# The order of the sync engine's work in a softmax attention: load, maxima, stores

## The reference

```
xn  = layernorm(x)                                   # 8 x 512 x 128
q, k, v = split(xn @ w_qkv + b_qkv)                   # per sequence 16 heads of 8
p   = softmax(q @ k.T * 8 ** -0.5)                    # 512 x 512 for each of 128 heads
s   = concat_heads(p @ v) @ w_proj + b_proj
g   = silu(top-2-of-8 experts(xn))
x   = x + s * g
```

## Time and profile before

| | us |
|---|---|
| median of 3 runs | 1123.48 (1121.21 to 1131.17) |
| profiled execution, own time | 1125.44 |
| profiled execution, span of the core | 1123.7 |
| PE busy | 986.1 (88%) |
| VectorE busy | 843.9 (75%) |
| ScalarE busy | 625.0 (56%) |
| GpSimd busy | 583.7 (52%) |
| mean granted clock of PE | 0.918 |
| attention (first plain scores to last transposed ones) | about 36 to 465 |

### The profile page before, as it was taken

How to read it: one execution, slowest core, us unless ns; L and a number is a source line. 1 busy time by engine, 2 the same in 40 slices (tenths; PEclk the granted TensorE clock), 3 DMA queues, 4 the chain that set the end, 5 groups by cost and what they waited for, 6 DMA issues and landing times. The chain is left out here.

```text
span 1123.7 us, 21302 instructions
## 1 busy us (share of the span) xinstructions
PE 986.1 (88%) x5638; PEld 640.7 (57%) x5638; DVE 843.9 (75%) x1901; ACT 625.0 (56%) x1247; POOL 583.7 (52%) x645
## 2 busy tenths in 40 slices
PE   5789999999999999999999945989987999999960
PEld 4443343443434444387888835656555888888850
DVE  7757798999999998045445538597883999998975
ACT  6126688788888877633323316223333677767752
POOL 7221786334435440025555546288882577667770
PEclk9558799999999999999999975699998999999985
DMA  6736656435344531245665643022242676677728
GB/s 210 287 115 197 192 149 201 124 124 179 123 159 140 160 114 41 85 136 172 193 187 178 190 114 88 20 67 69 66 154 76 178 217 204 202 213 199 216 72 231
DMA packets 121472, 169.76 MB, mean 151 GB/s; under 512 B 18801, under 2 KB 80594, under 8 KB 118354
## 3 DMA queue, kind: packets, MB, share of 16 engines
q1 hardware_dynamic: 94290, 110.94, 33.9%
q0 software_dynamic: 18688, 54.08, 14.1%
q10 hardware_dynamic: 8448, 4.20, 1.5%
HBM read 106.71 MB, written 63.76 MB: 152 GB/s over the span
## 5 line engine op out<-in xcount | busy, mean ns | idle before, releaser
L1660 DVE TENSOR_REDUCE nmax<-ps 128x1 f32<-128x512 f32 x512 | 324.2, 682 | 48.6 <-PE ps L1028 43.9
L1297 ACT ACTIVATE stage<-ps 128x512 f32<-128x512 f32 x512 | 274.6, 594 | 74.1 <-PE ps L1022 65.8
L846 POOL DMA_INDIRECT token_y<-stage,ids_now x184 | 184.9, 1005 | 141.4 <-DVE stage L1716 62.3
L1028 PE MATMUL ps<-stage,stage 32*128 32x512 f32 x512 | 190.0, 512 | 12.2 <-DVE nmax L1660 10.7
L1168 PE MATMUL ps<-stage,stage 128*128 128x128 f32 (+1 forms) x1288 | 172.5, 277 | 7.3 <-DVE stage L1780 3.9
L1022 PE MATMUL ps<-stage,stage 32*128 32x512 f32 x512 | 170.8, 487 | 8.9 <-DMA stage<-q_halves 3.9
L1168 PEld LDWEIGHTS ps<-stage,stage 128*128 128x128 f32 (+1 forms) x1288 | 164.2, 191 | 23.2 <-issue 8.6
L1022 PEld LDWEIGHTS ps<-stage,stage 32*128 32x128 f32 x512 | 70.1, 185 | 154.3 <-ACT stage L1297 123.3
L802 POOL DMA_INDIRECT slots_x<-xn,pos x128 | 132.1, 1032 | 38.7 <-issue 36.9
L324 PE MATMUL ps<-stage,stage 128*128 128x512 f32 x322 | 140.7, 437 | 4.2 <-issue 4.2
L1123 PE MATMUL ps<-stage,stage 128*32 128x512 f32 x1024 | 139.9, 619 | 0.0
(11 more groups left out here) (224 smaller groups left out, 1570.5 us busy)
## 6 DMA issues: line engine op xcount, KB each, us to landing
stage<-halves_w SPq DMA_DIRECT2D x23, 1024.0 KB
stage<-halves_w SPq DMA_DIRECT2D x23, 704.0 KB
stage<-slots_x SPq DMA_DIRECT2D x46, 260.0 KB
stage<-q_halves SPq DMA_DIRECT2D x32, 256.0 KB
halves_w<-stage POOLq DMA_DIRECT2D x16, 512.0 KB
k_halves<-stage SPq DMA_DIRECT2D x24, 256.0 KB
q_halves<-stage SPq DMA_DIRECT2D x24, 256.0 KB
stage<-k_halves SPq DMA_DIRECT2D x128, 48.0 KB
```

What stands on the lines that cost most here:

```text
L846: pool.indirect_dma_start(out=token_y, out_offset=bass.IndirectOffsetOnAxis(ap=ids_now[:, r, q:q + 1], axis=0), in_=ysb[:, r, q, :], in_of ...
L1028: pe.matmul(ps[:, (0, 1, 7)[bank_of(i)], :], head_rows(Qs, g2, j2)[:, t * P:(t + 1) * P], head_rows(Ks, g2, j2), start=True, stop=True).th ...
L1297: act.activation(probs[:, t % 2, j, :], ps[:, 2 + bank_of(i), :], ACT.Exp, scale=SCALE).then_inc(exp_set, 1)
L1660: dve.tensor_reduce(nmax[:, g % 2, at:at + 1], ps[:, (0, 1, 7)[bank_of(i)], :], AX, ALU.max, negate=True).then_inc(max_set, 1)
```

## The change

In SP's `attend` the three parts change places. Before: the halves' stores, the maxima's rows, the load. After: the load, the maxima's rows, the halves' stores. In `load_group` steps -1 and 0, which waited for no matmul before, now wait for the first plain score matmul of group u+1 (`s_mm`), by which time PE has passed its own wait for the earlier load of the other group of the same parity.

```
@@ load_group(u, g, bw)
                 if not (isinstance(u, int) and u < 1):
                     sp.wait_ge(st_mm, u * 16)
+                elif u >= -1:
+                    sp.wait_ge(s_mm, u * 16 + 17)
                 sp.wait_ge(halves_out, bw * 96 + 96)
...
             def attend(u, g, b, now):
+                if now.load:
+                    load_group(u, g, b if g == 0 else b + 1)
+                if now.low:
+                    max_rows(u + 1, (g + 1) % 2, (g + 1) % GROUPS)
                 if now.halves:
                     store_halves(b + 2)
-                if now.low:
-                    max_rows(u + 1, (g + 1) % 2, (g + 1) % GROUPS)
-                if now.load:
-                    load_group(u, g, b if g == 0 else b + 1)
```

## The result

The changed kernel takes **1114.82 us** (median of 4 runs, 1113.97 to 1116.72), the kernel before in the same comparison 1127.33 (4 runs, 1121.21 to 1131.88): a ratio of **0.9887**, 95% interval 0.9837 to 0.9936. The forecast was 1115. The gain is 12.5 us where 8.5 was forecast, since the kernel before is slower here than the 1123.48 that the forecast started from. The profiled execution took 1113.97, its span is 1112.2.

The account below looks back on a forecast made before the run. The prediction took PE to bound the attention, SP's queue mattering only where PE waits for its transfers or its clock changes. Terms of -10.1 and +1.1 us gave 1114.5 against the 1123.48 median, forecast 1115; 8-in-10 range 1110 to 1123.5.

Parts of the forecast that it names:

- The load first, -8.35 at step 2: Attention, start of step 2: earlier load removes PE's 2.12 us wait and about 6.2 us of work at lower clock.
- -1.28 at step 4: Attention, start of step 4: load issued some 8 us earlier in step 3 removes an excess of 1.28 us.
- -0.5 for the other two waits: Attention: PE's two remaining load waits, 0.5 us together, disappear.
- The rows of the maxima after the load, 0: SP's queue: 16 KB of rows now behind 448 KB of load still land in time; cost 0.
- The stores last, 0: SP's queue, every fourth step: 1.5 MB of halves' stores go out 5 to 9 us later; cost 0.
- The start, +1.1: Before step 0: group 2's early load delays POOL's stores that ScalarE waits for; +1.1 us, bounds 0 and 2.2.
- The sum: Whole kernel: -10.1 in the steps and +1.1 at the start, from the profiled 1125.44 to 1116.4; against the median 1114.5.
- Rival A: Attention: clock falls all the same, so only the waits go; 1120.7 us. Chance 0.16 together with a near relative.
- Rival B: Load for step 2: POOL's slot copies set its landing, so only some of the wait goes; 1122.6 us. Chance 0.08.
- Rival C: Steps after the halves' stores: PE waits for late rows of the maxima; 1131.7 us, at two places 1140. Chance 0.08.
- Rival D: Whole kernel: early load costs nothing and the median run before carried more clock falls than profiled; 1111 us. Chance 0.14.

Follow-up runs that it names:

- fill_the_wait: Kernel before, load still late, with nine matmuls nobody reads keeping PE busy ahead of the waits at steps 2, 10 and 18; 1118.27 us against 1116.02 before.
- before_again: The kernel before, unchanged, run for a second trace; it took 1126.72 us.
- one_load_first: Kernel before with the load ahead of the maxima's rows in steps 1, 9, 17 and 25 only; 1126.56 us against 1125.88 before.
- some_loads_first: Kernel before with the new order only in steps 1, 9, 17, 25 and the steps that store halves; 1104.31 us against 1117.68 before.
- load_stores_rows: Kernel before reordered to load, halves' stores, maxima's rows, so only the load's move; 1109.13 us against 1116.02 before.
- stores_last_only: Kernel before reordered to maxima's rows, load, halves' stores, so only the stores' move; 1110.55 us against 1116.02 before.
- after_again: The changed kernel, unchanged, for more times and a second trace; 1105.18 us against 1116.02 for the kernel before.
- start_load_late: Changed kernel with the load of step -1 put behind the maxima's rows; first 1116.35 us against 1125.88 before, run again 1103.42 against 1107.25 for the changed kernel.
- group 1: First of three sets of follow-up runs, each on one chip beside the kernel before, whose median here was 1125.88 us over 25 runs.
- one_load_late: Changed kernel with the load back behind the maxima's rows in steps 1, 9, 17 and 25 only; 1124.41 us against 1125.88 for the kernel before.

## Why the prediction was right, point by point

- **The load first, -8.35 at step 2.** Right in mechanism and size: between the transposes of steps 1 and 3 the trace lost 8.68 us, the clock stayed up, and the load went out at 92.71 where 92 was foretold. Of this, 0.3 is the yardstick: undisturbed, these steps take 23.6 us and not the 23.93 of later ones. By the trace of fill_the_wait the fall, not the wait, is the greater part, as the sum had split it.
- **-1.28 at step 4.** Right for the profiled execution (1.29), and wrong as a price. The term was read from an execution in which the wait of 1.26 us happened not to drop the clock. before_again and one_load_first have the fall there: from step 3 to 5 they take 29.88 and 33.56 us, against 23.88 in the trace after, so 6.0 and 9.7 us. This is the term that was mis-sized: the late loads together decide the median (some_loads_first), and one_load_first shows that mending the first alone does nothing measurable.
- **-0.5 for the other two waits.** They are gone, but the gain does not show: from the transpose of step 4 to that of step 30 it is 312.38 us, before 311.69.
- **The rows of the maxima after the load, 0.** Right: no wait for them in the trace. Their place ahead of the stores is what makes it so (load_stores_rows).
- **The stores last, 0.** It has no cost, and a gain was left out. Alone, with the load still behind the rows, it is worth 5.5 us by the median (stores_last_only), where the wait at step 4 is 0.78 us instead of 1.26 to 1.93. Behind the early load it is worth 3.9 by the median, not shown beyond spread, by keeping the rows clear of 1.5 MB (load_stores_rows). That both come from these waits is argued from one trace each.
- **The start, +1.1.** 1.17 between the two profiles, about 0.8 over all traces, and 0.6 to 0.9 more in the one trace with the load doubled. The turns that two queues take, cited from the Trainium skill's "DMA: Bandwidth & Descriptors", section "Queues, rings and completion order", fit this: POOL's stores end later with each load added. One trace of a late load (53.33) does not, and its cause is open. PE's step 0 was later by a further 0.4 us, since the 14 filler matmuls ahead of it took 5.90 instead of 5.54 us; that is spread, for unchanged they take 4.84 in before_again and 5.51 in after_again.
- **The sum.** The steps gave 9.3 instead of 10.1, and the end of the attention came 7.7 us earlier instead of 9.0. The span is 11.5 shorter. The missing 3.8 came after the attention: 1.3 at its edge, where before the projection ran at half the clock (the first line below, against the second, from after), and the rest in the stages behind. From the transpose of step 30 to the end it is 672.4 us before, 668.6 after, 667.1 in before_again, where the projection took 1.16 us too, and 672.5 in the first start_load_late; that part is spread between executions, not the change. So that the median came out at 1114.82, within 0.2 us of the forecast, is partly luck: the steps gave less than the sum, the end happened to give 3.8 more, and the kernel before was 1127.33 in this comparison instead of 1123.48.

```profile
475.66 2.08 PE L1099 MATMUL ps<-wproj,stage 128*128 128x128 f32 x8 [0.69 <-ACT stage L1323]
```

```profile
467.92 1.16 PE L1101 MATMUL ps<-wproj,stage 128*128 128x128 f32 x8 [0.69 <-ACT stage L1325]
```

- **Rival A** (the clock falls all the same) holds for single executions: falls without a load wait are seen in four traces of the first two groups. It does not hold for the median. The argument from the times that every run before had this fall is weaker than it looked: in group 1 the kernel before reached 1113.94 once. Whether that run was without the fall at step 2 no trace shows; all four traces with a late load there and PE idle have it. What varies is step 4: a fall in before_again at a wait of 1.93 us, none in before at 1.26. The prediction took a statement of the Trainium skill's "TensorE: Matmul & The Clock Gate", Part 1, for this; that statement is about where the clock rises in a first stretch of matmuls, and says nothing of whether it falls.
- **Rival B** fell: no load wait is left after the change.
- **Rival C** was rightly named and put at the wrong door. It needs the rows behind the stores of the same step, an order that the change avoids.
- **Rival D** may be partly the case: the medians are 10 to 12 us apart where the forecast had 8 to 9, and before_again has three falls where the first profile had one in the steps. With two traces of the kernel before, how many falls its median run has is not shown. The other half of D, a start without cost, was not the case in the profile.

## What to carry to other kernels

On a queue that waits in program order, put the transfer that is free to go ahead of the one whose data comes late, and bulk stores behind both; then ask what the early transfer now runs beside. Where PE bounds a stage, a wait of 1 to 2 us at it can cost several times its length through the clock, but not in every execution: price such a wait with and without the fall, and mend all its sites together, since one alone may show nothing. When times of one kernel spread over 20 us, one profile is one draw.

## What the runs showed of the hardware

In the attention's steps the clock fell to 0.50 behind all six waits of PE of 1.93 to 2.19 us for a transfer that the traces have. It fell behind one of 1.34 us (one_load_first) and stayed at 1.00 behind 1.26 (before), 1.29 (fill_the_wait, step 8) and 0.78 us (stores_last_only). It also fell without such a wait in five traces, as in steps 6 and 14 of two of them, where the longest gap of PE by the profile was 0.5 us, at the head of the step. What sets those off is open: in the trace after, PE waits 0.46 to 0.52 us for ScalarE in seven places and the clock stays. The falls lasted from about 6 us (one_load_late, from 354) to 24 us (one_load_first, from 84), by stretches of 2 us.

The column of the granted clock is not reliable before its first recorded change. In the trace after, it reads 1.00 all through the first 80 us, in the trace before 0.50 from 30 to 78; yet the same 512-column matmul took 0.80 us in both (at 82.16 in the trace before, where the column reads 1.00, it takes 0.50). First the stretch and the matmul after the change, then the matmul before:

```profile
38.00:50.00 12.00, 7.41 (x12) 3.37 (x12) 11.62 (x23) 0.42 (x1) 0.00 (x0) 1.00 1.02 409
```

```profile
48.86 0.80 PE L324 MATMUL ps<-xT_hi,wq_hi 128*128 128x512 f32 x1
```

```profile
48.04 0.80 PE L324 MATMUL ps<-xT_hi,wq_hi 128*128 128x512 f32 x1
```

So the mean clocks of two executions (0.918 before, 0.952 after) don't compare; durations of one matmul do.
